# Causal attention: row sums of two cells issued together, with four cells of probabilities kept

## The chip, the cores and the metric

The kernel runs on one core of one Trainium2 chip. The time is device microseconds of one execution; below, us is microseconds and PE, DVE, ACT, POOL and SP are TensorE, VectorE, ScalarE, GpSimd and SyncE.

## The reference

A block of two layers on x of 2048 rows by 128. The change touches only the causal attention of the second layer, which has 16 heads with queries and keys of 8 elements and values of 32:

```python
Q = _split_heads(x, H)
K = _split_heads(x @ Wk + bk, H)
V = _split_heads(x @ Wv + bv, H)
...
scores = jnp.einsum('bhqd,bhkd->bhqk', Q, K) + mask
attn = jax.nn.softmax(scores, axis=-1)
o = jnp.einsum('bhqk,bhkd->bhqd', attn, V)
o = o.transpose(0, 2, 1, 3).reshape(B, S, -1)
return x + jax.nn.gelu(o, approximate=False) @ Wf + bf
```

Everything ahead of it (a quantised feed-forward, linear attention, the same feed-forward again, a relu feed-forward) and behind it (the relu feed-forward again) is the same in both kernels.

## The kernel before

The causal attention is cut into 16 groups: four chunks `c` of 512 query rows, and in each chunk four groups of four heads. A group `g` (its chunk is `g // 4`) goes over its key tiles `kb` of 128 keys, `4*(c+1)` of them; one pair (group, key tile) is a **cell**, 160 in all. The last four cells of every group lie on the diagonal and have 512, 384, 256 and 128 query columns; all others have 512.

For one cell the kernel does this:

- `scores` (L1604), twice, two heads each: two bf16 matmuls of 50 rows by up to 512 columns, on the upper and the lower half of the array. Diagonal cells add a mask (L1610).
- `exponentials` (L920, ACT): one activation of up to 128x1024 from PSUM into `pr`, the ring of probabilities, for each `scores`.
- `values` (L1627): for four heads, probabilities times V in f32; 8 matmul instructions in the trace, into bank 6.
- `sums` (L1642): the same probabilities times a block of ones, which gives the row sums; again 8 matmul instructions, into bank 7. It is no longer than `values` and uses the same quarter-array tiles (128*32).

Beside this, the row maxima of a later group are found: `max` (L1569) is a score product of 512 columns or less for two heads, and DVE reduces it from PSUM (L1241). Over most of the kernel each cell carries two of them. From the last four cells of group 14 on, 20 cells, there are none.

**Banks.** `scores`, `max` and a few small products take turns in three sets of two PSUM banks (`SETS = 3`), strictly in the order of the program. An operation that takes a set waits on PE until the set's last reader is done, and that is the operation three takes before: ACT's exponential for a `scores`, DVE's reduction for a `max`. `values` waits for both exponentials of its cell (`s_p`).

**Order.** The steps stand in one list, `PLAN`, which every engine follows. In it `causal()` writes iteration `u` in two halves `i`: the first half has one `scores` of cell `u`, a `max`, and `values` of cell `u-1`; the second has the other `scores`, a `max`, and `sums` of cell `u-1`. Other steps (`e_k`, `wf`, `d_hidden` and so on) stand at the end of a half. PE works strictly in that order, so a matmul that waits holds up everything behind it.

**Ring.** `pr` has `RING = 3` places, one for each cell. `exponentials` of cell `u` waits for `sums` of cell `u - RING`.

Of the kernel before, what the change touches and what calls it, by code (L numbers as in the profile page):

```python
# [128 lines left out]
def build(nc, A, out):  # L129
    ctx = ExitStack()  # L130
    with ctx:
        def sb(name, shape, dt=F32):
            return ctx.enter_context(nc.sbuf_tensor(name, shape, dt))
# [6 lines left out]
        def bank(b, n=1):  # L140
            return psum[:, 512 * b:512 * (b + n)]
# [47 lines left out]
        rh = sb("rh", [P, 2, FJ, P])  # L189


        ARENA = 35424
        arena = sb("arena", [P, ARENA])

        def carver():
            at = [0]

            def carve(dims, dt=F32):
# [5 lines left out]
                at[0] += words  # L204
                assert at[0] <= ARENA, at[0]
                if dt != F32:
# [52 lines left out]
        KK = ce([PAIRS, S], BF16)  # L259
        QS = [ce([PAIRS, CH], BF16), ce([PAIRS, CH], BF16)]  # L260
        V = ce([TILES, H, VD])
        RING = 3
        pr = ce([RING, GP, 2, CH])
        GT = [ce([GPC, CH]), ce([GPC, CH])]
        DN = [ce([CH]), ce([CH])]
# [122 lines left out]
        def keys_and_values(first, end):  # L388

            out = []  # L390
            for i in range(first, end + 3):
                if i % TPC == SET_AT and first <= i < end:
                    out.append(("set_keys", i // TPC))
                for name, lag in (("e_stats", 0), ("e_norm", 1), ("e_turn", 2), ("e_k", 3), ("e_v", 3), ("split", 3)):
                    if first <= i - lag < end:
                        out.append((name, i - lag))
                        if name == "split" and (i - lag) % TPC == TPC - 1:
                            c = (i - lag) // TPC
                            out += [("store_parts", c), ("load_queries", c)]
            return out  # L400

        def causal():

            at = {}

            def put(u, *step):
                at.setdefault(u, []).append(step)

            for c in range(2, CHUNKS):
                lo, hi = GROUP_U[GPC * (c - 2)] + KEYS_START[c], GROUP_U[GPC * c - 1] - MAX_LEAD - KEYS_MARGIN  # L410
                steps = keys_and_values(TPC * c, TPC * c + TPC)
                for k, x in enumerate(steps):
                    put(lo + (hi - lo) * k // len(steps), *x)
            for g in range(2, MGROUPS):
                lo, hi = (GROUP_U[g - 1] - MAX_LEAD, GROUP_U[g] - MAX_LEAD)
                for k, x in enumerate(MAXES[g]):
                    put(lo + (hi - lo) * k // len(MAXES[g]), "max", *x)
                put(hi, "row_max", g)
                put(hi, "turn_max", g)
            for g in range(MGROUPS):  # L420
                c, end = g // GPC, GROUP_U[g + 1]
                last = c + 1 == CHUNKS
                if g + 1 < MGROUPS:
                    put(end + 2, "invert", g)
                    put(end + 2, "store_inverse", g)
                    put(end + 3, "spread_inverse", g)
                    put(end + NORM_AT, "norm", g)
                else:
                    for j in range(TPC):
                        put(end + 1 + j // 2, "invert_last", g, j)  # L430
                if g % GPC == GPC - 1:
                    put(end + (3 if last else GELU_AT), "gelu", c)
                    for j in range(TPC):
                        t = TPC * c + j
                        put(end + (4 if last else GELU_AT + 1 + j), "wf", t)
                        first = end + (5 if last else RELU_START + RELU_TILE * j)
                        for k, name in enumerate(("f_stats", "d_norm", "d_turn", "d_hidden", "d_out", "d_add")):
                            put(first + k, name, 2 * TILES + t)
            out = []
            for u in range(max(at) + 1):  # L440
                here = at.get(u, [])
                maxes = [x for x in here if x[0] == "max"]
                half = (len(maxes) + 1) // 2
                others = [x for x in here if x[0] not in ("max", "row_max", "gelu")]
                out += [x for x in here if x[0] in ("row_max", "gelu")]
                cut = (len(others) + 1) // 2
                for i in range(GP):
                    if u < len(CELLS):
                        out.append(("scores", GP * u + i))
                    out += maxes[half * i:half * (i + 1)]  # L450
                    if 0 < u <= len(CELLS):
                        out.append(("values" if i == 0 else "sums", u - 1))
                        g, kb = CELLS[u - 1]
                        if kb == TPC * (g // GPC + 1) - 1:
                            out.append(("take_o" if i == 0 else "take_d", g))
                    out += others[cut * i:cut * (i + 1)]

            ready, held = [], []
            for x in out:
                if held and x[0] in IN_SETS:  # L460
                    held[0][1] -= 1
                    if held[0][1] < 0:
                        ready.append(held.pop(0)[0])
                if x[0] != "d_add":
                    ready.append(x)
                if x[0] == "d_out":
                    held.append([("d_add", x[1]), 1])
            return ready + [x for x, _ in held]
# [8 lines left out]
                   early_q[3]] + [x for x in second if x not in early_q])  # L477
        main = len(PLAN)
        PLAN += causal()


# [14 lines left out]
        def both(x):  # L496

            b = 2 * set_of[x]
            return bank(b, 2).rearrange("p (a f) -> p a f", a=2), banks[b], banks[b + 1]
# [268 lines left out]
        def _(act):  # L768
# [144 lines left out]
            def exponentials(n):  # L913
# [3 lines left out]
                act.wait_ge(s_st, n + 1)  # L917
                if u >= RING:
                    act.wait_ge(s_dn, u - RING + 1)
                v.activation(pr[:, u % RING, pp, :, 0:CH - off], both(("scores", n))[0][:, :, off:CH], ACT.Exp  # L920
                             ).then_inc(s_p, 1)
# [362 lines left out]
        def _(pe):  # L1284
# [331 lines left out]
            def values(u):  # L1616
# [9 lines left out]
                for h in range(GH):  # L1626
                    last = mm(bank(O_BANK)[VD * h:VD * h + VD, off:CH], V[:, kb, GH * (g % GPC) + h, :],  # L1627
                              pr[:, u % RING, h // 2, h % 2, 0:CH - off], start=(kb == 0), stop=end,
                              skip_group_check=True)
# [4 lines left out]
            def sums(u):  # L1634
# [6 lines left out]
                for h in range(GH):  # L1641
                    last = mm(bank(D_BANK)[VD * h:VD * h + VD, off:CH], ones1[:, 0:VD],  # L1642
                              pr[:, u % RING, h // 2, h % 2, 0:CH - off], start=(kb == 0), stop=end,
                              skip_group_check=True)
# [75 lines left out]
```

## Time and profile before

| | |
|---|---|
| median of 3 runs | 1087.08 us (1086.32 to 1089.72) |
| profiled execution | 1085.72 us |
| its span, first to last instruction | 1083.9 us |
| PE busy | 914.4 us, 84% |
| DVE, ACT, POOL busy | 712.8, 511.7, 256.4 us |
| causal cells | from about 481 to 1053 us |

The span is what the trace covers; the execution's own time is 1.8 us longer. PE's busy time is the union of its matmuls, whose ends are modelled, so the distance between two starts is the better measure of what one costs.

### The profile page before, as it was taken

Reading aid. Unit: us, or ns where it says so; the run is one execution under the profiler, and the core shown is the slowest. Engines: PE = TensorE matmul, PEld = TensorE weight load, DVE = VectorE, ACT = ScalarE, POOL = GpSimd, SP = SyncE. Lnnn points to the kernel's source line nnn. Section 1 sums busy time; section 2 is a strip of 40 time slices with the busy share of each in tenths; the row PEclk is TensorE's granted clock in tenths of the full one; section 3 lists DMA queues with packets and bytes.
Section 4 is the critical chain, followed back from the end, with each engine's and each line's share of the span. In section 5 each row is a group of like instructions: output and inputs, shape, how many; then the busy total and the mean of one; then the engine's idle time right before and its main releaser. Section 6 shows DMA issues by size and latency. Waiting matters only on the chain.

```text
span 1083.9 us, 19987 instructions
## 1 busy us (share of the span) xinstructions
PE 914.4 (84%) x7353; PEld 454.6 (42%) x7353; DVE 712.8 (66%) x1676; ACT 511.7 (47%) x884; POOL 256.4 (24%) x404
## 2 busy tenths in 40 slices
PE   2788887778898866668889899899999989999986
PEld 1444445665677654443324333233322223332225
DVE  7899944467888776437755588556587747677002
ACT  1133332234453323225465556655655656666762
POOL 1546410035554559300312001112000000000000
PEclk9999998899999988859999999899999989999998
DMA  5200000000000001520001400000400000000000
GB/s 180 71 14 1 1 0 1 1 1 1 1 2 1 1 1 41 104 33 13 23 12 51 62 8 15 10 13 8 101 3 11 12 1 15 6 5 11 11 2 10
DMA packets 30934, 23.20 MB, mean 21 GB/s; under 512 B 9609, under 2 KB 27897, under 8 KB 30840
## 3 DMA queue, kind: packets, MB, share of 16 engines
q1 hardware_dynamic: 29928, 21.39, 8.6%
q8 instruction: 61, 1.00, 0.4%
q10 hardware_dynamic: 912, 0.54, 0.2%
q14 instruction: 33, 0.27, 0.1%
HBM read 17.32 MB, written 4.34 MB: 20 GB/s over the span
## 4 chain that ended last, share of the span: by engine, by line
PE 59%; DVE 16%; POOL 8%; ACT 7%; issue 6%; DMA 2%; SPq 1%; ACTq 0%; DVEq 0%; POOLq 0%
PE psum L1627 11%; PE psum L1642 10%; PE psum L1604 7%; DVE arena L1241 6%; PE psum L1569 5%; PE psum L1516 3%; PE psum L1363 3%; PE psum L1485 2%; PE psum L1322 2%; POOL rs L659 2%; PE psum L1527 2%; PE psum L1373 2%; ACT arena L920 2%; PE psum L1289 2%; PE psum L1656 1%
## 5 line engine op out<-in xcount | busy, mean ns | idle before, releaser
L1241 DVE TENSOR_REDUCE arena<-psum 128x2 f32<-128x1024 f32 (+2 forms) x320 | 336.0, 1063 | 150.7 <-PE psum L1569 78.3
L920 ACT ACTIVATE arena<-psum 128x1024 f32<-128x1024 f32 (+3 forms) x320 | 286.1, 897 | 173.6 <-PE psum L1604 97.0
L659 POOL TENSOR_TENSOR rs<-ve,mhalf 128x1 f32<-128x1 f32 x128 | 70.6, 557 | 363.2 <-DVE ve L1037 362.9
L1627 PE MATMUL psum<-arena 128*32 128x512 f32 (+3 forms) x1280 | 154.4, 555 | 1.3 <-ACT arena L920 1.3
L1642 PE MATMUL psum<-arena,ones 128*32 128x512 f32 (+3 forms) x1280 | 153.0, 551 | 0.0
L1569 PE MATMUL psum<-arena 48*128 48x512 bf16 (+3 forms) x640 | 114.9, 359 | 32.0 <-ACT arena L920 14.8
L1604 PE MATMUL psum<-arena 50*128 50x512 bf16 (+3 forms) x640 | 116.9, 361 | 11.1 <-ACT arena L920 4.1
L1604 PEld LDWEIGHTS psum<-arena 50*128 50x128 bf16 x640 | 31.2, 93 | 203.9 <-issue 134.9
L759 POOL TENSOR_TENSOR arena<-arena 128x512 f32<-128x512 f32 x15 | 19.1, 1273 | 229.2 <-DMA arena<-scr_sums 229.2
L892 ACT ACTIVATE rh<-psum,fb 128x128 f32<-128x128 f32 x128 | 36.4, 369 | 53.3 <-PE psum L1516 50.5
L1322 PE MATMUL psum<-WguT,xqT 128*128 128x352 f32 x128 | 54.2, 554 | 8.0 <-DVE hb L1068 7.1
L1569 PEld LDWEIGHTS psum<-arena 48*128 48x128 bf16 x640 | 36.4, 94 | 47.8 <-ACT arena L920 20.2
L1289 PE MATMUL psum<-bias_rows,onesb 128*128 128x128 bf16 (+1 forms) x128 | 37.4, 292 | 22.3 <-ACT rh L892 6.5
L1516 PE MATMUL psum<-xdT,fW 128*128 128x128 f32 x256 | 41.2, 312 | 7.7 <-ACT xdT L882 6.3
L663 POOL TENSOR_TENSOR xv<-xv,xm 128x128 f32<-128x128 f32 x32 | 20.4, 636 | 112.7 <-DVE xv L995 112.7
L1516 PEld LDWEIGHTS psum<-xdT,fW 128*128 128x128 f32 x256 | 36.1, 216 | 18.9 <-issue 9.3
L1627 PEld LDWEIGHTS psum<-arena 128*32 128x32 f32 x1280 | 25.5, 109 | 42.8 <-issue 38.1
L811 ACT ACTIVATE th<-psum 128x352 f32<-128x352 f32 x32 | 14.8, 463 | 54.8 <-PE psum L1322 54.8
L1413 PE MATMUL psum<-arena 128*128 128x256 f32 x128 | 38.2, 396 | 0.0
L1527 PE MATMUL psum<-fW,rh 128*128 128x128 f32 x256 | 38.1, 296 | 0.0
L1322 PEld LDWEIGHTS psum<-WguT,xqT 128*128 128x128 f32 x128 | 26.7, 229 | 22.3 <-issue 16.0
L1642 PEld LDWEIGHTS psum<-arena,ones 128*32 128x32 f32 x1280 | 25.5, 109 | 25.1 <-issue 20.3
(187 smaller groups left out, 1486.6 us busy)
## 6 DMA issues: line engine op xcount, KB each, us to landing
arena<-scr_parts SPq DMA_DIRECT2D x96, 64.0 KB
arena<-scr_sums SPq DMA_DIRECT2D x60, 64.0 KB, 2.0
scr_parts<-arena SPq DMA_DIRECT2D x12, 256.0 KB, 2.8
arena<-arena SPq DMA_DIRECT2D x124, 2.0 KB, 1.8
X<-in_L_attn_src_dram SPq DMA_DIRECT2D x4, 256.0 KB, 4.9
out_dram<-X SPq DMA_DIRECT2D x16, 64.0 KB, 1.6
arena<-in_c_zsel_dram SPq DMA_DIRECT2D x1, 512.0 KB, 3.7
arena<-in_L_attn_Wk_dram SPq DMA_DIRECT2D x1, 512.0 KB
```

The costliest lines, as they stand in the source:

```text
L659: v.tensor_tensor(rs[:, u, t:t + 1], ve[:, u, t:t + 1], mhalf[:, :], ALU.pow).then_inc(s_rstd[u], 1)
L920: v.activation(pr[:, u % RING, pp, :, 0:CH - off], both(("scores", n))[0][:, :, off:CH], ACT.Exp).then_inc(s_p, 1)
L1241: v.tensor_reduce(MXP[:, j, 2 * pp:2 * pp + 2, m], both(("max", g, pp, j, m))[0][:, :, 0:hi - lo], AX_X, ALU.max).then_inc(s_mxd, 1)
L1289: mm(o, onesb[:, 0:P], bias_rows[:, at:at + n], start=start, stop=False, skip_group_check=True)
L1322: last = mm(bank(b + k)[:, 0:GI], xqT[:, n % 2, :], WguT[:, k, :], start=True, stop=True)
L1413: last = mm(o, Wq[:, P * j:P * j + P], XNT[:, GRP * g:GRP * g + GRP], start=False, stop=True, skip_group_check=True)
L1516: last = mm(bank(b)[:, P * j:P * j + P], fW1[:, P * j:P * j + P], xdT[:, n % 2, :], start=True, stop=True)
L1527: last = mm(bank(b)[:, P:2 * P], rh[:, n % 2, j, :], fW2[:, j, :], start=False, stop=(j == FJ - 1), skip_group_check=True)
L1569: last = mm(o[:, par, 0:w], QS[c % 2][r, hp, P * j:P * j + P], KK[r, hp, lo:hi], start=True, stop=(m < c), skip_group_check=True)
L1604: last = mm(o[:, par, off:CH], KK[r, hp, P * kb:P * kb + P], QS[c % 2][r, hp, off:CH], start=True, stop=(kb < TPC * c), skip_group_check=True)
L1627: last = mm(bank(O_BANK)[VD * h:VD * h + VD, off:CH], V[:, kb, GH * (g % GPC) + h, :], pr[:, u % RING, h // 2, h % 2, 0:CH - off], start=( ...
L1642: last = mm(bank(D_BANK)[VD * h:VD * h + VD, off:CH], ones1[:, 0:VD], pr[:, u % RING, h // 2, h % 2, 0:CH - off], start=(kb == 0), stop=en ...
```

## The change

`sums` of a cell with an even key tile is no longer issued in its own iteration. It waits for the next one, and then `sums` of both cells are issued one behind the other. Every group has an even number of cells, so the pairs never cross a group. `RING` goes from 3 to 4, which makes `pr` 2048 words longer, and the arena 1728. Nothing is computed in another way and no instruction is added or taken away.

```diff
-        ARENA = 35424
+        ARENA = 37152
...
-        RING = 3
+        RING = 4
         pr = ce([RING, GP, 2, CH])
...
                     if 0 < u <= len(CELLS):
-                        out.append(("values" if i == 0 else "sums", u - 1))
                         g, kb = CELLS[u - 1]
+                        if i == 0:
+                            out.append(("values", u - 1))
+                        elif kb % 2:
+                            out += [("sums", u - 2), ("sums", u - 1)]
                         if kb == TPC * (g // GPC + 1) - 1:
                             out.append(("take_o" if i == 0 else "take_d", g))
```

In the changed kernel the lines of PE's steps are three further down: L1607 `scores`, L1572 `max`, L1578 its mask, L1630 `values`, L1645 `sums`. PE's order in group 14, before; each of the rows L1627 and L1642 is one whole `values` or `sums`:

```order
L1604 MATMUL psum<-arena 128x512 x2
L1569 MATMUL psum<-arena 128x512 x2
L1627 MATMUL psum<-arena 32x512 x4
L1604 MATMUL psum<-arena 128x512 x2
L1569 MATMUL psum<-arena 128x128 x2
L1575 MATMUL psum<-ident,mask_kq 128x64 x4
L1642 MATMUL psum<-arena,ones 32x512 x4
L1604 MATMUL psum<-arena 128x512 x2
L1569 MATMUL psum<-arena 128x512 x2
L1627 MATMUL psum<-arena 32x512 x4
L1604 MATMUL psum<-arena 128x512 x2
L1569 MATMUL psum<-arena 128x512 x2
```

The next row of before is the second L1642. The same place in the changed kernel:

```order
L1607 MATMUL psum<-arena 128x512 x2
L1572 MATMUL psum<-arena 128x512 x2
L1630 MATMUL psum<-arena 32x512 x4
L1607 MATMUL psum<-arena 128x512 x2
L1572 MATMUL psum<-arena 128x128 x2
L1578 MATMUL psum<-ident,mask_kq 128x64 x4
L1607 MATMUL psum<-arena 128x512 x2
L1572 MATMUL psum<-arena 128x512 x2
L1630 MATMUL psum<-arena 32x512 x4
L1607 MATMUL psum<-arena 128x512 x2
L1572 MATMUL psum<-arena 128x512 x2
L1645 MATMUL psum<-arena,ones 32x512 x8
```

The L1642 between the first `max` with a mask and the next `scores` is gone from its place, so that two `scores` and two `max` follow each other with no f32 product between them; both sums now stand at the end (x8).

What PE waits for there, in the changed kernel; a row ends with the semaphores that its first instruction waits for, `probs` is raised by ACT's exponentials and `mx_reduced` by DVE's reductions:

```order
L1607 MATMUL psum<-arena 128x512 [waits mx_reduced]
L1607 MATMUL psum<-arena 128x512
L1572 MATMUL psum<-arena 128x256 [waits probs]
L1572 MATMUL psum<-arena 128x256
L1578 MATMUL psum<-ident,mask_kq 128x64 x4
L1607 MATMUL psum<-arena 128x512 [waits mx_reduced]
```

The waits are those of before, since the sets are handed out in the same order: a `scores` waits for the reduction of the `max` three takes back, a `max` for the exponential of the `scores` three takes back. What moved is how much of PE's work lies between the two.

## Rows read from the trace of the kernel before

**Rows 1.** The page: busy time of each engine, and the chain by engine.

```profile
PE 914.4 (84%) x7353; PEld 454.6 (42%) x7353; DVE 712.8 (66%) x1676; ACT 511.7 (47%) x884; POOL 256.4 (24%) x404
...
PE 59%; DVE 16%; POOL 8%; ACT 7%; issue 6%; DMA 2%; SPq 1%; ACTq 0%; DVEq 0%; POOLq 0%
```

**Rows 2.** Busy by window: the window and its length, PE, PEld, DVE, ACT, POOL, clock, DMA.

```profile
481.00:1053.00 572.00, 533.13 (x5199) 183.71 (x5198) 355.53 (x466) 344.17 (x467) 54.05 (x77) 0.96 0.08 19
...
505.00:530.00 25.00, 20.06 (x263) 8.55 (x263) 22.54 (x39) 12.52 (x19) 6.85 (x8) 1.00 0.10 24
```

**Rows 3.** Timeline of PE, cells of 512 columns with maxima: start, length.

```profile
997.42 0.39 PE L1604 MATMUL psum<-arena 50*128 50x512 bf16 x2
997.64 0.38 PE L1569 MATMUL psum<-arena 48*128 48x512 bf16 x2
997.96 1.06 PE L1642 MATMUL psum<-arena,ones 128*32 128x512 f32 x8
998.95 0.39 PE L1604 MATMUL psum<-arena 50*128 50x512 bf16 x2
```

**Rows 4.** Timeline of ACT there: the exponential of the scores at 997.42.

```profile
997.85 1.02 ACT L920 ACTIVATE arena<-psum 128x1024 f32<-128x1024 f32 x1 [0.51 <-PE psum L1604]
```

**Rows 5.** Timeline of DVE there: the reduction of the max at 997.64.

```profile
998.07 1.23 DVE L1241 TENSOR_REDUCE arena<-psum 128x2 f32<-128x1024 f32 x1 [0.31 <-PE psum L1569]
```

**Rows 6.** Timeline of PE at a group's end: a max held by an exponential.

```profile
965.52 0.39 PE L1604 MATMUL psum<-arena 50*128 50x512 bf16 x2
...
966.06 0.42 PE L1627 MATMUL psum<-arena 128*32 128x128 f32 x8
966.42 0.39 PE L1604 MATMUL psum<-arena 50*128 50x512 bf16 x2
967.12 0.39 PE L1569 MATMUL psum<-arena 48*128 48x512 bf16 x2 [0.31 <-ACT arena L920]
```

**Rows 7.** Timeline of PE, cells without maxima.

```profile
1021.00 0.39 PE L1604 MATMUL psum<-arena 50*128 50x512 bf16 x2
1021.32 1.06 PE L1642 MATMUL psum<-arena,ones 128*32 128x512 f32 x8
1022.31 0.39 PE L1604 MATMUL psum<-arena 50*128 50x512 bf16 x2
```

**Rows 8.** Timeline of PE, the last values and sums (128 columns).

```profile
1052.48 0.43 PE L1627 MATMUL psum<-arena 128*32 128x128 f32 x8
1052.72 0.40 PE L1642 MATMUL psum<-arena,ones 128*32 128x128 f32 x8
```

**Rows 9.** Timeline of PE: two maxima in a row (x4), then values.

```profile
803.67 0.60 PE L1569 MATMUL psum<-arena 48*128 48x512 bf16 x4
804.20 0.64 PE L1627 MATMUL psum<-arena 128*32 128x256 f32 x8
```

**Rows 10.** Timeline of all engines, cells of 384 columns.

```profile
959.56 0.34 PE L1604 MATMUL psum<-arena 50*128 50x384 bf16 x2
...
959.99 0.81 ACT L920 ACTIVATE arena<-psum 128x768 f32<-128x768 f32 x1 [0.73 <-PE psum L1610]
...
961.49 0.85 PE L1627 MATMUL psum<-arena 128*32 128x384 f32 x8
...
962.27 0.28 PE L1604 MATMUL psum<-arena 50*128 50x256 bf16 x2
```

**Rows 11.** Timeline of PE: three short waits close together.

```profile
535.90 0.30 PE L1536 MATMUL psum<-ident,xe 128*128 128x128 f32 x1 [0.42 <-DVE arena L1241]
...
537.03 0.39 PE L1604 MATMUL psum<-arena 50*128 50x512 bf16 x2 [0.47 <-DVE arena L1241]
...
538.63 0.61 PE L1569 MATMUL psum<-arena 48*128 48x512 bf16 x2 [0.41 <-ACT arena L920]
```

**Rows 12.** Busy by window, as in rows 2, just behind them.

```profile
539.00:540.50 1.50, 1.50 (x10) 0.20 (x8) 1.22 (x1) 0.89 (x1) 1.36 (x3) 0.50 0.06 12
540.50:542.00 1.50, 1.50 (x6) 0.65 (x3) 0.01 (x1) 0.00 (x0) 0.34 (x1) 0.54 0.02 1
```

## Prediction

> **What bounds the kernel now.** I read the page first. PE is busy for 84% of the span, and the chain that ended last runs through PE for 59% of it [rows 1]. The cells lie between 481 and 1053 us, so the next view is the busy time of that stretch: PE 533.1 of 572 us, DVE 355.5, ACT 344.2 [rows 2]. PE sits idle there for 39 us in all, so whatever PE's order costs or saves comes out in the time nearly whole. One stretch is different: from 505 to 530 DVE is busy for 22.5 of 25 us and PE for 20.1 [rows 2].
>
> Then the timeline of PE, for the rhythm. From start to start, `scores` to `max` takes 0.22 to 0.23 us, `max` to an f32 product 0.31, and that product to the next `scores` 1.00; a half-iteration is 1.54 us [rows 3]. Without maxima it is 0.32 + 1.00 = 1.32 [rows 7]. I call the f32 products V (`values`) and Σ (`sums`), the others S (`scores`) and M (`max`).
>
> The third thing to read is how long a set of banks stays taken. The exponential starts 0.43 us behind its S and takes 1.02 [rows 3, 4]. When PE has nothing to do but wait for it, the rows show the whole distance: S at 965.52, and the M that needs its set at 967.12, marked as idle until ACT: **1.60 us** [rows 6]. So 0.15 of it lies between the exponential's end and PE. For a reduction it is 0.43 + 1.23 [rows 3, 5] and, I take it, the same 0.15: **1.81 us** from M to the S that needs its set. In the rhythm of before, PE does M, an f32 product and the next S between an S and the M that waits for its exponential: 0.23 + 0.31 + 1.00 + 0.23 = 1.77, just above 1.60. This is why PE hardly waits: each f32 product covers one exponential. In the cells without maxima V needs the exponentials of its cell: from S over Σ and the next S that is 0.32 + 1.00 + 0.32 = 1.64, again just above 1.60.
>
> **What the change saves.** No work goes away, but there are fewer changes between bf16 and f32 products. Of two f32 products in a row the first takes less: with 128 columns V to Σ is 0.24 us [rows 8], while V to S is 0.36 [rows 6], so 0.12 less. With 512 columns I take the same, 0.88 instead of 1.00. Two bf16 products in a row: two M and the way to V are 0.53 us, so M to M is 0.53 - 0.31 = 0.22 [rows 9], where M to an f32 product is 0.31, so 0.09 less. Together 0.21 us for each pair of cells, and with 80 pairs 16.8 us. That is the whole gain on offer. The unknown is whether the 0.12 holds at 512 columns; between 0 and 0.25 (twice the row) the gain is 7 to 28 us.
>
> The Trainium skill, TensorEngine Tiling (Array Packing), section Key Properties, says that changing the tiling mode drains the engine. The trace agrees in kind: S and M use half-array tiles, V and Σ quarter tiles, and each change costs about a tenth of a microsecond. By that rule alone the change is a gain, which is the second rival below.
>
> **What it costs.** The Σ that goes away from its place was what covered an exponential. I lay out one pair from the first S behind a double Σ, at time 0, with the distances above; full cells with maxima:
>
> S0 0; M0 0.23; V 0.54; S1 1.54; M1 1.77. Then S2 follows with no Σ between. It could start at 1.99 and needs M0's reduction, 0.23 + 1.81 = 2.04. M2 could start at 2.27 and needs S1's exponential: 1.54 + 1.60 = **3.14**. PE stands still for 0.87 us. Then V 3.45, S3 4.45, M3 4.68 (S2's exponential follows S1's on ACT and is done near 4.1), Σ 4.99, Σ 5.87, next S 6.87.
>
> Before, the same work takes 4 x 1.54 = 6.16. So a pair costs +0.71: 0.92 of waiting less 0.21. The long double Σ gives nothing back, since nothing was late there. Other kinds of pairs:
>
> - No maxima: S0 0, V 0.32, S1 1.32, S2 1.54, then V needs S1's exponential at 1.32 + 1.60 = 2.92 instead of 1.86; S3 3.92, Σ 4.24, 5.12, end 6.12, against 5.28. +0.84.
> - The cells of 512 and 384 columns on the diagonal: the exponential is 0.81 and starts 0.43 behind its S, V or Σ of 384 columns is 0.78 [rows 10]. The gate is at 1.55 + 0.43 + 0.81 + 0.15 = 2.94 where M2 could start at about 2.2. Laid out in the same way the pair ends at 6.2 against 5.64. I take +0.55.
> - The cells of 256 and 128 columns: exponentials are short, but so is the work between M0 and S2, and M0's reduction holds S2 by some 0.6. DVE is close to its limit there in both kernels. I take +0.3, between 0 (DVE sets the pace) and 0.6.
>
> The count: 160 cells are 80 pairs. 16 groups have one pair of each diagonal kind, 32. The other 48 are full, of which 6 (group 15) have no maxima. 42 x 0.71 + 6 x 0.84 + 16 x 0.55 + 16 x 0.3 = 29.8 + 5.0 + 8.8 + 4.8 = 48.4 us. Off this comes what fills the gaps: in the order, 6 pairs have another product just where PE would wait (three `wf`, two `d_hidden`, one `e_k`), which hides from some 0.3 us up to the whole 0.87; I take off 3.7 us, an estimate. Another 3 us for the cells between 505 and 530, where PE already waits for DVE.
>
> **The ring of four** costs nothing that I can find, and gives nothing: with three places, an exponential would wait for a Σ that PE has already passed when it reaches the `scores` in question. If it did matter, it could only show as ACT waiting, and ACT has over 200 us of slack in the stretch.
>
> **The sum.** 48.4 - 3.7 - 3 = 41.7 us on the profiled execution's 1085.7 gives 1127.4. That execution lies 1.4 us below the median of the runs, so **1129 us**.
>
> **The rivals.**
>
> *The clock falls.* Three waits of 0.42, 0.47 and 0.41 us within 3.2 us [rows 11] are followed by a granted clock of 0.50, that is 1.2 GHz instead of 2.4 [rows 12]. On the other hand the stretch 505 to 530 has PE busy at 80% and a clock of 1.00 [rows 2]. The changed kernel waits 0.92 of 6.87 us, in one piece mostly, which lies between these two. Most at risk are group ends, where two or three waits come close together. If every one of the 16 brings one more stretch of some 3 us at half clock [rows 12], in which PE does half its work, each costs 1.5 us: +24, or 1153 us. What speaks against it is that PE's idle share, 13%, is below the 20% of that stretch. The Trainium skill, TensorE: Matmul & The Clock Gate, section A second HAM failure mode, describes a kernel with short idle gaps between groups of matmuls whose clock goes up and down; it would be this rival. Chance 0.18.
>
> *No new wait, only the gain.* If PE does not stand still at M2, 16.8 us are won: 1087.1 - 16.8 = 1070 us. The mechanism has its place at S2, M2 and V behind each odd cell. It decides where an S's set comes free within 0.69 us (S1 to M2 unhindered is 0.23 + 0.22 + 0.23), and a gain begins below about 0.9 us. The rows say 1.60, and the same order of takes already shows this very wait at a group's end, where a V of 128 columns is too short a cover [rows 6]. This is also what the drain rule taken alone gives. Chance 0.05.
>
> *Half hidden.* Some of the waits replace waits of before (39 us of idle in the stretch), or the double Σ lets ACT and DVE catch up so that the waits of group ends vanish. Half the waiting (80 pairs near 0.4) gives 0.4 - 0.21 = +0.2 each, 1103 us. Chance 0.09.
>
> *It comes out even*, saving and waiting alike: 1087 us. Chance 0.03.
>
> **How the numbers follow.** A measurement of this kernel can tell about 0.3%, some 3 us, from no change. The forecast has 0.65, and slower in all is 0.65 + 0.18 + 0.09 = 0.92; same 0.03; faster 0.05. The range begins at 1110: the last diagonal kind at 0 takes off 4.8 us, a saving of 0.25 + 0.09 for each pair another 10.4, and 4 us stand for more waits of before that the new ones replace. It ends at 1156, the clock rival and 3 us over. Below it lie half hidden, even and gain (0.17), above it a clock that falls oftener.
>
> **What the profile would show.** PE idle in front of L1572 with ACT L923 as releaser, about 0.9 us, once in two cells, some 45 times; in the cells without maxima about 1.06 us in front of L1630. The double Σ, x8 and x8, with 1.88 us to the next start. PE's total idle in the cells near 39 + 60 us. ACT and DVE as busy as before. S and M in a row 0.22 apart. If instead the distance from S to the gated M is well under 1.60 us, the waiting is over-priced; if the starts of bf16 products are spread at half speed behind the waits, it is the clock. The prediction is wrong if PE's idle time doesn't rise.

## The result, and the profile after

The changed kernel takes 1119.49 us (median of 4 runs, 1117.20 to 1125.52) against 1087.22 us (4 runs): a ratio of 1.030, with a 95% interval of 1.0252 to 1.0348. It is slower by 32 us where 42 were forecast (1129 us), inside the stated range. The profiled execution took 1117.20 us, its span is 1115.4.

The page of the changed kernel, the lines that answer to [rows 1], and its clock by slice:

```profile
PE 909.4 (82%) x7335; PEld 468.0 (42%) x7353; DVE 713.2 (64%) x1676; ACT 508.0 (46%) x884; POOL 256.6 (23%) x404
...
PEclk9999998999999988578989999999999999999998
...
PE 54%; DVE 20%; ACT 9%; POOL 8%; issue 6%; DMA 2%; SPq 1%; ACTq 0%; DVEq 0%; POOLq 0%
```

The slices of low clock (tenths of full speed) lie mostly ahead of the cells and at their start, where the kernel before has them too. The chain tells the direction: PE lost 5 points, DVE won 4 and ACT 2. The work is the same. The busy view of the stretch of the cells, which answers to [rows 2]; it is 602 us long instead of 572:

```profile
481.00:1083.00 602.00, 523.28 (x5176) 192.79 (x5184) 354.62 (x466) 340.00 (x466) 54.04 (x77) 0.97 0.08 18
```

PE is idle for 78.72 us where it was 38.87, 39.85 more. Its busy time fell by 9.85. Together that is the 30.0 us between the two stretches. How much of the 9.85 comes from fewer changes of product isn't shown, since the two traces also differ in the places where the clock is halved, and by 23 matmul records. The clock is 0.97, before 0.96. The view of the waits in that stretch says who holds PE (in total, times, longest):

```profile
PE psum L1572 <- ACT arena L923: 35.9, 52, 3.1
PE psum L1572 <- DVE arena L1244: 8.8, 17, 0.8
PE psum L1630 <- ACT arena L923: 8.7, 12, 0.9
```

In the kernel before the same three were 14.8, 7.3 and 1.3 us.

One regular pair in the timeline of PE (S is L1607, M L1572, V L1630, the double sums L1645 x16), and the exponentials of ACT beside it:

```profile
1003.17 0.39 PE L1607 MATMUL psum<-arena 50*128 50x512 bf16 x2
1003.40 0.38 PE L1572 MATMUL psum<-arena 48*128 48x512 bf16 x2
1003.71 1.07 PE L1630 MATMUL psum<-arena 128*32 128x512 f32 x8
1004.71 0.39 PE L1607 MATMUL psum<-arena 50*128 50x512 bf16 x2
...
1005.20 0.39 PE L1607 MATMUL psum<-arena 50*128 50x512 bf16 x2
1006.31 0.39 PE L1572 MATMUL psum<-arena 48*128 48x512 bf16 x2 [0.72 <-ACT arena L923]
1006.63 1.06 PE L1630 MATMUL psum<-arena 128*32 128x512 f32 x8
1007.63 0.39 PE L1607 MATMUL psum<-arena 50*128 50x512 bf16 x2
1007.86 0.38 PE L1572 MATMUL psum<-arena 48*128 48x512 bf16 x2
1008.17 1.92 PE L1645 MATMUL psum<-arena,ones 128*32 128x512 f32 x16
1010.02 0.39 PE L1607 MATMUL psum<-arena 50*128 50x512 bf16 x2
```

```profile
1005.14 1.94 ACT L923 ACTIVATE arena<-psum 128x1024 f32<-128x1024 f32 x2 [0.51 <-PE psum L1607]
```

From the S at 1004.71 to the M that takes its set, at 1006.31, is 1.60 us, the distance of [rows 6]; the first exponential of the two (x2) starts at 1005.14 and takes 1.02, and M follows 0.15 behind its end. The next S is done long before, and PE can do nothing but wait. (The bracket shows 0.72, since the matmul ahead counts as busy for 0.39.) The pair takes 6.85 us. The double sums take 1.85 instead of twice 1.00.

Without maxima:

```profile
1045.67 0.39 PE L1607 MATMUL psum<-arena 50*128 50x512 bf16 x2
1045.99 1.06 PE L1630 MATMUL psum<-arena 128*32 128x512 f32 x8
1046.99 0.61 PE L1607 MATMUL psum<-arena 50*128 50x512 bf16 x4
1048.50 1.07 PE L1630 MATMUL psum<-arena 128*32 128x512 f32 x8 [0.90 <-ACT arena L923]
1049.49 0.39 PE L1607 MATMUL psum<-arena 50*128 50x512 bf16 x2
1049.81 1.93 PE L1645 MATMUL psum<-arena,ones 128*32 128x512 f32 x16
1051.67 0.39 PE L1607 MATMUL psum<-arena 50*128 50x512 bf16 x2
```

Here V is held, 1.51 us behind its S at 1046.99. The pair takes 6.00 us against 5.27.

The 32 us can be counted over the pairs of both traces, from the first `scores` of an odd cell to that of the next odd cell. Full pairs behind the first of their group became longer by 0.64 to 0.86 us each in 30 of 36 cases. By kind: 42 full pairs +16.9 us, 6 full ones without maxima +3.6, 15 with 512 and 384 columns +8.7, 15 with 256 and 128 columns +1.0 (the last two pairs of all are not in this count).

Most pairs that aren't bare, because another product stands between, pay too, but not to the exponential alone. In this one `d_hidden` (L1519, until 937.14) has taken a set, and ACT reads it as `rh`:

```profile
937.14 0.39 PE L1607 MATMUL psum<-arena 50*128 50x512 bf16 x2
937.37 0.38 PE L1572 MATMUL psum<-arena 48*128 48x512 bf16 x2
...
938.44 0.39 PE L1607 MATMUL psum<-arena 50*128 50x512 bf16 x2 [0.63 <-ACT rh L895]
939.44 0.39 PE L1572 MATMUL psum<-arena 48*128 48x512 bf16 x2 [0.61 <-ACT arena L923]
```

The S at 938.44 is the third take behind `d_hidden` and waits for that reader, and the M behind it for the exponential. In the stretch PE waits for `rh` in front of a `scores` 7 times, 4.6 us in all; before it never did. In front of `scores` it waits 7.4 us for DVE's reductions, before 2.6.

### The profile page after: what moved, and what is told of

Its sections match the earlier page's. It is cut to its first block, busy times and chain, and to the rows that moved or that the text cites. A ratio compares the mean times of both kernels' runs of the same rounds, so it can differ in the third digit from the quotient of the medians.

```text
span 1115.4 us, 19967 instructions
## 1 busy us (share of the span) xinstructions
PE 909.4 (82%) x7335; PEld 468.0 (42%) x7353; DVE 713.2 (64%) x1676; ACT 508.0 (46%) x884; POOL 256.6 (23%) x404
## 4 chain that ended last, share of the span: by engine, by line
PE 54%; DVE 20%; ACT 9%; POOL 8%; issue 6%; DMA 2%; SPq 1%; ACTq 0%; DVEq 0%; POOLq 0%
PE psum L1630 10%; PE psum L1645 10%; DVE arena L1244 6%; PE psum L1607 5%; ACT arena L923 5%; PE psum L1572 5%; PE psum L1519 3%; PE psum L1530 2%; POOL rs L662 2%; PE psum L1488 2%; PE psum L1366 2%; PE psum L1325 2%; PE psum L1659 2%; PE psum L1553 1%; PE psum L1376 1%
## 5 line engine op out<-in xcount | busy, mean ns | idle before, releaser
L923 ACT ACTIVATE arena<-psum 128x1024 f32<-128x1024 f32 (+3 forms) x320 | 280.6, 896 | 197.9 <-PE psum L1607 112.2
L1630 PE MATMUL psum<-arena 128*32 128x512 f32 (+3 forms) x1280 | 153.5, 552 | 8.7 <-ACT arena L923 8.7
L1572 PE MATMUL psum<-arena 48*128 48x512 bf16 (+3 forms) x640 | 114.6, 357 | 50.3 <-ACT arena L923 35.9
L1645 PE MATMUL psum<-arena,ones 128*32 128x512 f32 (+3 forms) x1280 | 134.9, 540 | 0.0
L1607 PE MATMUL psum<-arena 50*128 50x512 bf16 (+3 forms) x640 | 115.1, 359 | 19.1 <-DVE arena L1244 7.4
L1607 PEld LDWEIGHTS psum<-arena 50*128 50x128 bf16 x640 | 31.9, 93 | 159.3 <-issue 89.6
L1572 PEld LDWEIGHTS psum<-arena 48*128 48x128 bf16 x640 | 35.8, 95 | 73.8 <-ACT arena L923 48.1
L1645 PEld LDWEIGHTS psum<-arena,ones 128*32 128x32 f32 x1280 | 34.0, 111 | 58.1 <-issue 53.9
L1519 PE MATMUL psum<-xdT,fW 128*128 128x128 f32 x256 | 42.9, 322 | 7.5 <-ACT xdT L885 5.9
L1292 PE MATMUL psum<-bias_rows,onesb 128*128 128x128 bf16 (+1 forms) x110 | 29.9, 272 | 21.0 <-ACT rh L895 6.5
L1630 PEld LDWEIGHTS psum<-arena 128*32 128x32 f32 x1280 | 25.5, 109 | 49.0 <-issue 34.5
L1519 PEld LDWEIGHTS psum<-xdT,fW 128*128 128x128 f32 x256 | 37.8, 226 | 18.1 <-ACT xdT L885 9.1
L814 ACT ACTIVATE th<-psum 128x352 f32<-128x352 f32 x32 | 14.8, 463 | 55.2 <-PE psum L1325 55.2
```

Of the source, the lines that this page charges most:

```text
L1519: last = mm(bank(b)[:, P * j:P * j + P], fW1[:, P * j:P * j + P], xdT[:, n % 2, :], start=True, stop=True)
L1572: last = mm(o[:, par, 0:w], QS[c % 2][r, hp, P * j:P * j + P], KK[r, hp, lo:hi], start=True, stop=(m < c), skip_group_check=True)
L1607: last = mm(o[:, par, off:CH], KK[r, hp, P * kb:P * kb + P], QS[c % 2][r, hp, off:CH], start=True, stop=(kb < TPC * c), skip_group_check=True)
```

## Experiments

The first four are each compared with 23 runs of the kernel before on the same chip (median 1083.41 us), the next four with 18 (1083.60), and the last two with 22 (1085.11).

**The ring alone.** `RING = 4` and `ARENA = 37152` in the kernel before, no pairing.

> The kernel before with RING = 4 and the larger arena, the sums left where they were. My theory (PE waits because the cover between a scores product and the taker of its set is gone): the ring has no part in it, 1087 us, within 0.3%. Rival (the longer arena or the later reuse of places costs or gives something): more than 3 us from 1087.

Measured: 1085.90 us, ratio 1.0011 (0.9977 to 1.0044). The ring of four alone makes no difference that these runs can tell.

**The pairing alone.**

```diff
-        ARENA = 37152
+        ARENA = 35424
...
-        RING = 4
+        RING = 3
```

> The changed kernel with RING = 3 and the old arena: only the pairing. My theory: the same as the changed kernel, 1119 us within 0.4%, with the 0.7 us waits in the same places, since the exponential of a cell needs a sums that stands ahead of its scores in PE's order with three places too. Rival (the ring is needed for the pairing): clearly slower than 1119, with ACT waiting for L1645's line.

Measured: 1118.08 us, ratio 1.0322 (1.0272 to 1.0372), the changed kernel's. The same wait, at the same place and as long, in its trace:

```profile
1006.09 0.39 PE L1607 MATMUL psum<-arena 50*128 50x512 bf16 x2
...
1007.69 0.39 PE L1572 MATMUL psum<-arena 48*128 48x512 bf16 x2 [0.72 <-ACT arena L923]
```

The two together split the change: the loss is all the pairing's. Against the 23 runs it is 34.7 us, a little more than the 32 against the four runs of the result.

**Pairs in the last 20 cells only.**

```diff
+                        elif u - 1 < 140:
+                            out.append(("sums", u - 1))
                         elif kb % 2:
                             out += [("sums", u - 2), ("sums", u - 1)]
```

> The changed kernel with pairs only in the last 20 cells, which carry no maxima. There the trace of the changed kernel shows 6.00 us for a full pair against 5.27 before, six times, 0.56 for one diagonal pair and some 0.2 for the rest. My theory, that each pair pays by itself: 1087.2 + 6 x 0.73 + 0.56 + 0.2 + 0.67 or about 1092.5 us (+0.5%). Rival (the loss comes from maxima and DVE, or from the clock): 1087 or less, because 20 cells without maxima gain 0.2 us a pair by fewer changes of product.

Measured: 1090.79 us, ratio 1.0054 (1.0022 to 1.0085), expected 1.005. There are no maxima for DVE to reduce there, so the loss doesn't need them. Of the six full pairs four take 6.00 us for 5.27 and one 6.06 for 5.39, but the first takes 6.63 for 6.60 (the expectation had 0.73 for all six). One of the four, on PE:

```profile
1019.82 0.39 PE L1609 MATMUL psum<-arena 50*128 50x512 bf16 x2
...
1022.64 1.06 PE L1632 MATMUL psum<-arena 128*32 128x512 f32 x8 [0.90 <-ACT arena L925]
...
1025.82 0.39 PE L1609 MATMUL psum<-arena 50*128 50x512 bf16 x2
```

**The held max behind the values.** In the first half of each even iteration the maxima go behind `values`:

```diff
-                    out += maxes[half * i:half * (i + 1)]
+                    late = i == 0 and 0 < u <= len(CELLS) and CELLS[u - 1][1] % 2 == 1
+                    if not late:
+                        out += maxes[half * i:half * (i + 1)]
...
+                    if late:
+                        out += maxes[half * i:half * (i + 1)]
                     out += others[cut * i:cut * (i + 1)]
```

> The changed kernel, with the max in the gap (the one that waits for ACT) moved behind the values that follows it. Theory A, the one of my prediction: both the max (by its set, 1.60 us behind the scores) and the values (by the probabilities, 1.51 us behind it in the cells without maxima) wait for the same exponential, so nearly all of the wait stays and goes over to values: the next S comes at 1.54 + 1.51 + 1.00 + 0.23 = 4.28 instead of 4.46, 0.18 us less for each of 42 + 14 pairs with maxima, about 1110 us. Rival B, that only the set of banks is the gate: the wait goes away, and the kernel is 0.7 us x 50 = 35 us faster than the changed one, 1085 us or less.

Measured: 1128.41 us, ratio 1.0413 (1.0365 to 1.0462): 10 us slower than the pairing alone (1118.08), which neither theory had. The trace parts it in two. In pairs with no other step in them V now waits in M's stead, and a pair takes 6.66 instead of 6.85, -0.19 where A said -0.18. The wait didn't go away, so B falls.

```profile
1008.28 0.39 PE L1611 MATMUL psum<-arena 50*128 50x512 bf16 x2
...
1009.79 1.06 PE L1634 MATMUL psum<-arena 128*32 128x512 f32 x8 [0.62 <-ACT arena L927]
```

But where another product, such as the turn of `xd`, stands behind V, four takes of a set now come in a row:

```profile
938.80 0.39 PE L1576 MATMUL psum<-arena 48*128 48x512 bf16 x2
939.12 0.33 PE L1513 MATMUL psum<-ident,xd 128*128 128x128 f32 x1
939.38 0.39 PE L1611 MATMUL psum<-arena 50*128 50x512 bf16 x2
940.60 0.39 PE L1576 MATMUL psum<-arena 48*128 48x512 bf16 x2 [0.83 <-DVE arena L1248]
```

The last M needs the set of the first and waits for its reduction, 1.80 us behind it. Such pairs became up to 1.1 us longer. So it is the same rule again, with the other reader, and it was missed because the expectation was worked out on a bare pair.

**Exponentials of half the columns**, in the kernel before and in the pairing with three places. The other half of the probabilities isn't computed, so the output isn't the attention's:

```diff
-                v.activation(pr[:, u % RING, pp, :, 0:CH - off], both(("scores", n))[0][:, :, off:CH], ACT.Exp
+                w = (CH - off) // 2
+                v.activation(pr[:, u % RING, pp, :, 0:w], both(("scores", n))[0][:, :, off:off + w], ACT.Exp
```

> The kernel before with exponentials of the first half of each row of columns only; the other half of the probabilities stays whatever lies in the ring, so the output is not the attention's. It is the control of the next run. The exponential takes 0.60 us instead of 1.02. PE has hardly any wait for ACT in the regular cells, so my theory says 1080 to 1087 us, only the waits at the ends of groups shrink. A rival by which the exponentials bound the kernel says 1050 or less.

> The pairing (with three places) and the same half exponentials, output as little the attention's. Theory A: the wait in a pair is the exponential's length less what covers it. With 0.60 us the gate is 0.43 + 0.60 + 0.15 = 1.18 behind the scores instead of 1.60, so a full pair takes 6.43 instead of 6.85, 0.27 more than before instead of 0.69, and the kernel is some 14 us slower than its control instead of 32. Rival (the loss is a fixed cost of the order, say in the double sums or in the clock): again 32 us slower than the control.

Measured: 1073.45 us for the control (0.9874, 0.9817 to 0.9931) and 1096.19 for the pairing (1.0108, 1.0074 to 1.0142). The control gained more than I said; in its trace PE's waits for the exponential in front of `max` fell from 14.8 us to 6.2. The difference, 22.7 us, lies midway between the two theories, and the control's four runs alone spread from 1061.1 to 1075.9, so the totals decide nothing. The pairs do decide. A regular pair of the second kernel:

```profile
1000.56 0.39 PE L1608 MATMUL psum<-arena 50*128 50x512 bf16 x2
...
1001.04 0.39 PE L1608 MATMUL psum<-arena 50*128 50x512 bf16 x2
1001.73 0.39 PE L1573 MATMUL psum<-arena 48*128 48x512 bf16 x2 [0.29 <-ACT arena L924]
```

From S to the held M is 1.17 us (A said 1.18), the wait in the bracket 0.29 instead of 0.72: 0.43 less for an exponential 0.42 shorter. The pair takes 6.42 (A: 6.43), without maxima 5.57 against the control's 5.27. In a bare pair the length of the exponential sets the wait, one for one.

It doesn't in all. Of the 31 full pairs with maxima behind the first of their group, 11 are still 0.72 to 0.87 us longer than the control's. They carry another product or a third `max`. Here is the pair of 937.14 above, with half the columns:

```profile
925.09 0.39 PE L1608 MATMUL psum<-arena 50*128 50x512 bf16 x2 [0.63 <-ACT rh L895]
925.67 0.39 PE L1573 MATMUL psum<-arena 48*128 48x512 bf16 x2 [0.19 <-ACT arena L924]
```

The wait for `rh` is as long as with full exponentials. The one for the exponential fell by 0.42. But the kernel before waits 0.32 us for the exponential there too, the control doesn't, and so the loss stays 0.86. In a pair of group 11 with a third `max` PE waits for DVE's reductions instead, 0.74 and 0.51 us, whether the exponential is long or short. That theory A counted with bare pairs alone is one reason why the totals lie above its 14 us.

**The pair of sums at another place.** Iteration `u` with `kb` even: S M V S M; with `kb` odd: S, both sums, M S M V. Four places; `others` behind V.

```diff
+                    if u % 2 and i == 0 and 3 <= u <= len(CELLS) + 1:
+                        out += [("sums", u - 3), ("sums", u - 2)]
+                        g, kb = CELLS[u - 2]
+                        if kb == TPC * (g // GPC + 1) - 1:
+                            out.append(("take_d", g))
                     out += maxes[half * i:half * (i + 1)]
-                    if 0 < u <= len(CELLS):
+                    if i == u % 2 and 0 < u <= len(CELLS):
+                        out.append(("values", u - 1))
...
-                    out += others[cut * i:cut * (i + 1)]
+                    if i == u % 2:
+                        out += others
```

> The sums paired as in the changed kernel, four places, but the pair moved between the products that need cover: in an even cell S M V S M, in the next cell S, both sums, M S M V; other steps behind V. There are never more than three takers of a set between two f32 products. By the distances of the traces a full pair is S 0, M 0.23, V 0.54, S 1.54, M 1.77, S 2.04, sums 2.35 and 3.21, M 4.21, S 4.43, M 4.66, V 4.97, next S 5.97 (6.02 where the set's reduction holds it), against 6.16 before; without maxima 5.27 becomes 5.06. My theory: 42 x 0.14 to 0.19 + 6 x 0.21 and nothing at the group ends, about 8 us faster than before, 1079 us (-0.7%), 40 us faster than the changed kernel. Rival (pairing loses wherever the pair stands): 1087 or more.

Measured: 1094.49 us, ratio 1.0090 (1.0057 to 1.0124). Some 25 us better than the changed kernel, but not better than before. The pair itself came as laid out, 6.00 us from S to S and no wait, with the same double sums:

```profile
1002.57 0.39 PE L1610 MATMUL psum<-arena 50*128 50x512 bf16 x2
1002.79 0.38 PE L1575 MATMUL psum<-arena 48*128 48x512 bf16 x2
1003.05 0.39 PE L1610 MATMUL psum<-arena 50*128 50x512 bf16 x2
1003.37 1.92 PE L1648 MATMUL psum<-arena,ones 128*32 128x512 f32 x16
...
1008.57 0.39 PE L1610 MATMUL psum<-arena 50*128 50x512 bf16 x2
```

So that the sums stand side by side is not the loss, the hole they leave is. Without maxima a pair takes 5.03 instead of 5.27. One thing that this order loses elsewhere is a long wait of DVE, whose order still had the reciprocal of the row sums at its old place, while the sums end half an iteration later:

```profile
785.42 0.25 DVE L1265 RECIPROCAL arena<-arena 128x16 f32<-128x16 f32 x1 [6.03 <-DMA arena<-arena]
```

**The same with three places.**

> The same with three places. Here the sums that free a place stand behind the scores whose exponential needs it, so the fourth place should matter for the first time: the exponential of the S at 2.04 waits for the first sums, until 3.21 + 0.5, which is over 1.1 us later than it could start; M at 4.66 then waits for it until 3.7 + 1.0 + 0.15 = 4.9, 0.2 to 0.3 us in each full pair. My theory: 8 to 15 us slower than with four places. Rival (the ring never matters): the same as with four.

Measured: 1100.29 us, ratio 1.0140 (1.0097 to 1.0183), some 6 us more than with four (1.0090, intervals overlap). In the timeline of ACT the exponential of the S at 986.96 starts at 988.48, 1.52 us behind it instead of 0.43, released by the first half of the sums:

```profile
988.48 1.02 ACT L926 ACTIVATE arena<-psum 128x1024 f32<-128x1024 f32 x1 [0.55 <-PE psum L1648]
```

So in this order the ring of three does delay an exponential, as expected. But it rarely costs the 0.2 to 0.3 us that were expected of every full pair: in group 14 the full pairs are as long as with four places, within 0.03 us, the second pair of groups 8, 9, 12 and 13 pays 0.16 to 0.28, and the whole stretch of cells is 3.2 us longer.

**The reciprocal later.** `invert`, `store_inverse`, `spread_inverse` and `norm` each one iteration later in the spread kernel (`end + 3`, `end + 3`, `end + 4`, `end + NORM_AT + 1`).

> The spread pairs of before, and DVE's reciprocal of the row sums, its store, its load and POOL's product each one iteration later. In the trace of the spread kernel DVE waits 31.8 us in all for the gathered sums, against 21.1 before, once for 6.0 us, behind which a scores product waited 4.7 us: the sums of a group now end one half-iteration later, and the reciprocal was still at its old place in DVE's order. My theory: that is the main part of what the spread kernel lost, and the time goes from 1094 to 1086 us or so. Rival (group ends themselves, +1.4 us in each last diagonal pair, are what it lost): no change from 1094.

Measured: 1091.76 us, ratio 1.0066 (1.0041 to 1.0091). DVE's wait for the gathered sums fell to 18.7 us, and group 10, where the long wait was, went from 49.8 to 42.5 us. But the total moved by about 0.2%, within the intervals: either that stall is not the main part of what the spread order loses, or the gain was lost again elsewhere. The traces show such a place. Groups 5 and 6 took 5.0 us more than in the trace of the spread kernel, and between them PE waits for a DMA:

```profile
605.14 0.61 PE L1610 MATMUL psum<-arena 50*128 50x512 bf16 x2 [4.65 <-DMA arena<-arena]
```

The clock behind it, from 605 to 610, is 0.50. This one wait was 1.4 us in the spread trace and 0.3 to 3.9 in four traces with the order of before, so it is in part chance. Whether the later reciprocal has lengthened it isn't shown. The rival fits no better: the last diagonal pair of groups 12 and 13 is 1.2 and 1.4 us longer, and the first pair of the next group as much shorter. Against the kernel before, groups 2, 6, 7, 8 and 11 lose 1.6 to 4.5 us each. In 2 every cell carries four maxima, in 6, 7 and 11 about half of them carry three, and in 6, 7 and 8 other products stand between. What holds PE there, beside that wait, stays open.

**Spread order in the last four groups only**, with the later reciprocal there, the order of before in groups 0 to 11:

```diff
+                    wide = u >= GROUP_U[12]
...
+                    if i and 0 < u <= GROUP_U[12]:
+                        out.append(("sums", u - 1))
```

> The spread order with the later reciprocal in groups 12 to 15 only (64 of the 160 cells), the order of before in the others. In the traces the spread kernel took 1.37, 1.26, 0.78 and 1.67 us less than before in those four groups. My theory: 5 us less than before, plus one new wait of 0.7 us where the two orders meet, so about -4.4 us, a ratio of 0.996. Rival (short gains don't add up, or the clock takes them back): a ratio of 1.00 or more.

Measured: 1082.05 us (12 runs) against 1085.11 (22 runs), ratio 0.9969 (0.9947 to 0.9992), where 0.996 was expected. It beats both kernels, by little. In its trace the groups 12 to 15 (up to the end of the last sums) take 60.0, 56.6, 45.5 and 40.2 us against 60.8, 57.4, 46.2 and 41.4, together 3.5 us less. The 1.67 us that the expectation has for group 15 were counted to the start of the last sums, which come earlier as a pair; to their end it is 1.2.

## Why the prediction was right, and where it was off

**The mechanism was right.** Each step of the laid-out pair has its row: the gap from S to the M that takes its set is 1.60 us in both kernels, the pair 6.85 us for 6.87, the diagonal pair of 512 and 384 columns 6.17 against 5.54 in clean places, +0.63 for +0.55. That the wait is ACT's exponential was argued before; for the bare pair it is now shown, by its length (half the columns take 0.43 us off it) and by its place (the spread order has the double sums and no wait). In the pairs with more in them the same rule holds with other readers, `rh` and DVE's reductions. The prediction had counted other products as something that hides the wait.

**The size was 6 to 10 us too large.** A single trace of the kernel before carries chance: the last pair of group 5 takes 11.39 us in it, and 6.35, 7.68 and 8.80 in three other traces with the same order there, for one DMA wait of 3.9, 0.3, 1.6 and 2.8 us. So the sum is set beside two couples of traces, the result's and that of the first two experiments, which have the same two orders with the other ring. The difference by kind of pair, in us:

| pairs | forecast | before to changed | ring of four alone to pairing alone |
|---|---|---|---|
| 12 full, first of groups 4 to 15 | 8.7 | 0.1 | 1.6 |
| 31 other full with maxima | 22.0, less 6.7 for fillers and DVE | 16.8 | 16.5 |
| 5 other full without maxima | 4.2 | 3.6 | 3.6 |
| 16 of 512 and 384 columns | 8.8 | 9.2 | 9.4 |
| 16 of 256 and 128 columns | 4.8 | 1.5 | 5.1 |
| sum | 41.7 | 31.2 | 36.2 |

What was mis-sized:

- *42 x 0.71 + 6 x 0.84, all full pairs alike.* The first full pair of a group did not pay 0.71. This is the one term that is too large in both couples, by 7.1 to 8.5 us. In the kernel before, both `scores` of a group's first cell are followed by a held M, one of which is [rows 6]. In the changed kernel the second is covered by the double sums of the last diagonal cells:

```profile
987.59 0.39 PE L1607 MATMUL psum<-arena 50*128 50x512 bf16 x2
988.29 0.39 PE L1572 MATMUL psum<-arena 48*128 48x512 bf16 x2 [0.31 <-ACT arena L923]
988.61 0.86 PE L1645 MATMUL psum<-arena,ones 128*32 128x256 f32 x16
989.40 0.39 PE L1607 MATMUL psum<-arena 50*128 50x512 bf16 x2
989.69 0.39 PE L1572 MATMUL psum<-arena 48*128 48x512 bf16 x2
```

 So "the long double Σ gives nothing back, since nothing was late there" holds inside a group and fails at its end. In undisturbed places such a pair pays 0.27 us, 0.44 less than 0.71. In group 4 it became 1.1 to 1.2 us shorter in both couples: its clock is 0.82 with the order of before, [rows 12] being part of it, and 1.00 with the pairs. The 1.1 us that group 11 gained is chance: the pair takes 8.65 us at a clock of 0.72 in the trace of before, but 6.74 at 1.00 in that of the ring of four alone, and 7.58 at 1.00 with the pairs in both.

- *The last diagonal kind, 16 x 0.3*, was not mis-sized, as far as can be told: +0.33 to +0.38 in clean places and 5.1 us in the second couple. The 1.5 of the first couple is mostly that DMA wait at the end of group 5, which was 3.9 us and then 2.3.
- *The gate of V.* I took 1.60 us, the distance of an M. V waits for the probabilities and comes 1.51 behind its S, so a pair without maxima paid 0.73 and not 0.84 (the rest of the difference is in the double sums).
- *The 0.12 of the double sums* is 0.15 at 512 columns (1.85 for 2.00).
- *"PE's total idle near 39 + 60".* It is 79 us: some new waits replaced old ones, as under the rival "half hidden". This is so at the group ends. The two longest pairs, with the long waits of the gelu steps, 14.35 and 13.81 us before, even became 1.3 and 1.5 us shorter in the first couple, 1.9 and 1.0 in the second.
- *"Within 0.69 us"* (the rival without a wait) should be 0.23 + 0.22 + 0.23 = 0.68. Nothing hangs on it.

The 6.7 us taken off for fillers and for the cells between 505 and 530 us came out near, with 5.2 and 5.5 in the full pairs, but partly by luck. Over 4 of these come from the two gelu pairs, which the prediction didn't name. The 8 pairs of groups 0 to 3, in which that stretch lies, paid 2.9 and 3.7 us, where 3.4 less 3 was forecast.

**The rivals.** The clock did not fall on the whole: its mean in the stretch is 0.97 with 13% of the time idle, where it was 0.96 with 7%. It moved in places, down from 1.00 to 0.86 between 505 and 530 us and up from 0.83 to 1.00 between 534 and 544, in both couples of traces. The failure that the Trainium skill describes in TensorE: Matmul & The Clock Gate, A second HAM failure mode, a clock that short idle gaps send up and down, did not set the time here. The rival of the gain without a wait did not come either, but its term is real: the trace has 0.09 and 0.15 us less where products of one kind follow each other, and a pair of the spread order keeps both. That agrees in kind with the drain of the Trainium skill's TensorEngine Tiling (Array Packing), Key Properties; since the number type changes together with the tiling here, no run tells which of the two costs the time. The ring was rightly put at nothing, and the reason given (the sums in question stand ahead of the scores in PE's order) is what the spread order with three places undoes.

## What to carry to other kernels

Before two products of one kind are put side by side to save changes of mode, look at what the one that is moved was covering. With the three sets of banks here, three takes between two long products made no wait in a bare pair (the spread order) and four did, for whichever reader came last. Count the takes in every kind of iteration, also in those that carry other products, and compare the work between a take and the third one behind it with the time of the reader and its hand-over. The double step itself is harmless if it stands where cover is wanted; moving a step also moves what other engines wait for behind it, as DVE's reciprocal here. And before a term is called mis-sized by the difference of two traces, look at a second trace of each order: one DMA wait differed by 3.6 us between traces of the same order.

## What the runs showed of the hardware

- The hand-over had the same price for three readers: exponential or reduction starts 0.43 us behind the start of a 512-column product, and the product that takes its set starts 0.15 us behind its end. With 1.02, 0.60 and 1.23 us of reading this gave 1.60, 1.17 and 1.80.
- A product that waits for the probabilities and not for a set started 1.51 us behind the `scores`, where one that waits for the set started 1.60 behind.
- The change from f32 products on quarter tiles back to bf16 on half tiles costs 0.12 us (128 columns) to 0.15 us (512), the other way 0.09.
- The kernel before ranged from 1078.5 to 1091.0 us in 23 runs, its mean granted clock from 0.957 to 0.940, the slower ones mostly at the lower clock. Of a change below 0.3% only many runs can tell.
